# Linear attention and mixture of experts on one core: router in four column groups, part of the first two batches' masks and remainders on ScalarE and GpSimd, batch 0 loaded in halves

## What is computed

```python
x = L0_attn_x                                  # (16, 512, 256)
x = x + attn(layernorm(x), Wq, Wk, Wv, Wo)
x = x + ffn(layernorm(x), ...)

# attn: 16 heads of 16; q, k = elu(proj) + 1; v = proj
#   kv_sum += k_i v_i^T ; k_sum += k_i
#   out_i = (q_i kv_sum) / (q_i . k_sum + 1e-8) ; return out @ Wo.T

# ffn: 8 routed experts of width 128 and one shared one
scores   = sigmoid(x @ gate_w.T)               # 8 per token
scores_c = scores + correction_bias
# the best 2 of 4 pairs of experts, then the best 4 experts of those
topk_w   = chosen scores / their sum * 2.5
out      = sum_e cw[e] * (silu(x @ Wg[e]) * (x @ Wu[e])) @ Wd[e] + shared expert
```

## Time and profile before

| | |
|---|---|
| median of 3 runs | 1066.31 us (1066.13 to 1067.27) |
| the profiled execution's own time | 1064.54 us |
| its span, first to last instruction | 1062.7 us |
| PE busy | 1035.6 us, 97% |
| DVE busy | 857.4 us, 81% |
| POOL, ACT busy | 515.6 and 421.1 us, 49% and 40% |
| granted TensorE clock | 0.998 of full speed over the span |

### The profile page before, as it was taken

The page is one execution under the profiler, slowest core; times in us unless marked ns, Lnnn a source line. Parts: engine busy times, 40 slices in busy tenths (PEclk is TensorE's granted clock), DMA queues, the critical chain, the costliest instruction groups (busy, mean ns, idle before and its releaser), DMA issues.

```text
span 1062.7 us, 22269 instructions
## 1 busy us (share of the span) xinstructions
PE 1035.6 (97%) x8481; PEld 878.6 (83%) x8481; DVE 857.4 (81%) x1856; ACT 421.1 (40%) x751; POOL 515.6 (49%) x423
## 2 busy tenths in 40 slices
PE   7899999999999999999999999999999999999998
PEld 6777888888788888878888887888878888888887
DVE  5999978798787979878798897879978798786553
ACT  5544342443435244352443434334342443431222
POOL 4223435535355463544635355463544645353556
PEclk9999999999999999999999999999999999999999
DMA  6001424444252453324434252453425444240512
GB/s 222 2 21 52 99 57 124 81 110 100 56 135 61 110 119 91 100 54 136 82 110 101 56 134 60 110 120 84 106 50 141 81 110 101 56 113 24 135 40 85
DMA packets 234889, 96.46 MB, mean 91 GB/s; under 512 B 161440, under 2 KB 217248, under 8 KB 234784
## 3 DMA queue, kind: packets, MB, share of 16 engines
q1 hardware_dynamic: 234784, 95.04, 35.5%
HBM read 66.57 MB, written 28.44 MB: 89 GB/s over the span
## 4 chain that ended last, share of the span: by engine, by line
PE 48%; DVE 9%; DMA 6%; issue 5%; POOL 4%; ACT 3%; SPq 1%; DVEq 0%; ACTq 0%; POOLq 0%
PE bank L918 30%; PE y_bank L918 11%; PE bank L1025 3%; DMA x_dram<-blocks 2%; PE bank L1039 2%; POOL h_lo L683 2%; DMA expo<-x_dram 2%; POOL et L679 1%; DVE stats L698 1%; ACT h_hi L637 1%; SPq L496 1%; DVE blocks L778 1%; PE bank L1012 1%; DMA cw_all<-cw_dram 1%; DVE et L895 1%
## 5 line engine op out<-in xcount | busy, mean ns | idle before, releaser
L683 POOL TENSOR_TENSOR h_lo<-et,h_hi 128x512 fp32r<-128x512 f32 x144 | 183.2, 1287 | 169.6 <-ACT h_hi L637 169.2
L918 PE MATMUL bank<-xt_hi,wg_hi 128*128 128x512 f32 x576 | 234.6, 407 | 0.5 <-DVE scores L805 0.3
L918 PE MATMUL bank<-xt_hi,wg_lo 128*128 128x512 f32 x576 | 228.9, 397 | 0.0
L918 PE MATMUL bank<-xt_lo,wg_hi 128*128 128x512 f32 x576 | 227.4, 395 | 0.0
L679 POOL TENSOR_TENSOR et<-et,cw_all 128x512 f32<-128x512 f32 x128 | 164.5, 1292 | 99.5 <-DVE et L901 66.1
L805 DVE TENSOR_TENSOR scores<-bank,cst 128x512 f32<-128x512 f32 x256 | 163.9, 679 | 25.4 <-PE bank L1025 20.5
L637 ACT ACTIVATE h_hi<-et 128x512 fp32r<-128x512 f32 x144 | 88.6, 627 | 212.7 <-POOL et L679 184.8
L918 PE MATMUL y_bank<-wd_hi,h_hi 128*128 128x256 f32 x576 | 164.8, 286 | 0.1
L895 DVE SCALAR_TENSOR_TENSOR et<-et,bank 128x512 f32<-128x512 f32 x144 | 97.0, 682 | 81.1 <-ACT et L628 79.7
L918 PE MATMUL y_bank<-wd_lo,h_hi 128*128 128x256 f32 x576 | 161.1, 280 | 0.0
L918 PE MATMUL y_bank<-wd_hi,h_lo 128*128 128x256 f32 x576 | 161.0, 280 | 0.0
(11 more groups left out here) (130 smaller groups left out, 1918.2 us busy)
## 6 DMA issues: line engine op xcount, KB each, us to landing
cw_all<-cw_dram SPq DMA_DIRECT2D x128, 256.0 KB, 3.7
x_dram<-blocks SPq DMA_DIRECT2D x112, 128.0 KB, 3.3
x_in<-in_x SPq DMA_DIRECT2D x16, 512.0 KB, 5.2
out_y<-x_mid SPq DMA_DIRECT2D x32, 256.0 KB, 3.8
num_t<-x_dram SPq DMA_DIRECT2D x15, 512.0 KB, 4.0
expo<-x_dram SPq DMA_DIRECT2D x13, 512.0 KB, 4.1
k_dram<-blocks SPq DMA_DIRECT2D x52, 96.0 KB, 2.7
k_tok<-k_dram SPq DMA_DIRECT2D x13, 384.0 KB, 3.4
```

Source lines behind the costliest of these rows:

```text
L683: nc.gpsimd.tensor_tensor(h_lo[:, i % HR, :], et[:, i % ET, :], h_hi[:, i % HR, :].bitcast(f32), ALU.subtract).then_inc(h_lo_done, 1)
L918: ins = nc.tensor.matmul(dst, l, r, start=first and n == 0, stop=last and n == 2, skip_group_check=shared)
```

## The change

- The router's matrix (padded with zeros from 8 to 32 columns, `wr`, whole fp32) is now the weights, and the transposed tokens move: one matmul for each block of tokens and half of the features, each block in its own column group, 32 rows of the bank. From batch 1 on the tokens are read whole from `landed[1]` (the tile num_t, as the DMA left it): 8 matmuls. In batch 0, which PE transposes, `xt_hi` and `xt_lo` are read as fp32 one after the other: 16 matmuls. `spread`, which overwrites num_t, waits for the router too.
- DVE turns the bank's 128x128 into `logit` by 32x32 transposes, and `cw` (padded to 32 columns a block, zeroed once by POOL) into `cw_t` (128x128) in the same way at the end of `rank1`. The step `weights_turn` is gone on PE and ACT. The store is 64 KB instead of 16; a load reads four pieces of 512 B for each partition instead of one of 2 KB.
- The tile of equalities (`eq`) is gone: it is written into `cmp` and multiplied there.
- In batches 0 and 1 the masks 1, 3, ... 15 are a copy by ACT, which frees the bank, and the multiplication by POOL from SBUF. `values` waits for both. `at_lo` of these two batches is made by POOL.
- Piece 1's low part goes from DVE to POOL. Batch 0 is loaded by two DMAs of 256 KB, and the statistics of the first half start on the first.
- The tables of order and of banks are others, all through. PE's `warm` transposes are 68 instead of 79.

```diff
@@ FIRST, "PE" @@
-        turn.0.0 turn.1.0 warm.21.0 q.0.0 k.0.0 q.1.0 v.1.0 warm.9.0 k.1.0 scores.0.0 warm.12.0 v.0.0
-        k_turn.1.0 scores.1.0 warm.8.0 turn.0.1 state.1.0 k_turn.0.0 state.0.0 values.0.0 turn.1.1 warm.9.0
-        inter.0.0 scores.2.0 inter.1.0 values.1.0 scores.3.0 k.0.1 k.1.1 values.2.0 values.3.0 inter.2.0
-        inter.3.0 q.0.1 wo.0.0 wo.1.0 q.1.1 scores.0.1 v.1.1 k_turn.0.1 v.0.1 warm.8.0 turn.2.0 turn.3.0
+        turn.0.0 turn.1.0 warm.17.0 k.0.0 q.0.0 k.1.0 v.0.0 q.1.0 k_turn.0.0 k_turn.1.0 v.1.0 scores.0.0
+        warm.10.0 scores.1.0 turn.1.1 state.0.0 warm.10.0 values.0.0 turn.0.1 inter.0.0 scores.2.0 inter.1.0
+        k.0.1 state.1.0 k.1.1 values.1.0 scores.3.0 warm.9.0 q.0.1 values.2.0 inter.2.0 inter.3.0 k_turn.0.1
+        values.3.0 q.1.1 scores.0.1 v.1.1 scores.1.1 wo.0.0 wo.1.0 v.0.1 scores.2.1 values.0.1 k_turn.1.1
+        warm.11.0 turn.3.0 turn.2.0 values.1.1 scores.3.1 router.0.0 warm.11.0 state.0.1 gate.2.0 gate.0.0
...
@@ load of batch 0 @@
+                    sp.dma_start(x_in[0][:, 0:HALF, :], x_v[0][:, 0:HALF, :]).then_inc(x_half, 16)
+                    sp.dma_start(x_in[0][:, HALF:SUBS, :], x_v[0][:, HALF:SUBS, :]).then_inc(x_loaded[0], 16)
@@ cw_load @@
-                    sp.dma_start(cw_all[:, i % CW, :], cw_dram[b % 2, i].partition_broadcast(P))\
+                    sp.dma_start(cw_all[:, i % CW, :].rearrange("p (g t) -> p g t", t=P),
+                                 cw_dram[b % 2].rearrange("(g e) t -> e g t", e=RG)[i].partition_broadcast(P))\
@@ ACT @@
+                elif name == "mask":
+                    act.wait_ge(filled, FILLED["scores", i, b])
+                    nc.scalar.activation(scores[:, i % SM, :, :].rearrange("p h q -> p (h q)"),
+                                         bank[BANK["scores", i]][:, :], ACT.Copy)\
+                        .then_inc(drained[BANK["scores", i]], 1)
@@ POOL @@
+                elif name == "mask":
+                    pool.wait_ge(drained[BANK["scores", i]], USES["scores", i, b])
+                    nc.gpsimd.tensor_tensor(scores[:, i % SM, :, :], scores[:, i % SM, :, :],
+                                            causal.unsqueeze(1).broadcast_to([P, 4, P]), ALU.mult).then_inc(masked, 1)
+                elif name == "at":
+                    nc.gpsimd.tensor_tensor(at_lo[:, i, :], num_t[:, i, :], at_hi[:, i, :].bitcast(f32), ALU.subtract)\
+                        .then_inc(at_lo_pool, 1)
@@ DVE, router and rank1 @@
-                    nc.vector.tensor_reduce(
-                        logit[:, :, :].rearrange("p s e -> p (s e)"),
-                        bank[BANK["router", 0]][:, 0:SUBS * 2 * E].rearrange("p (s t e) -> p s e t", s=SUBS, t=2),
-                        AX.X, ALU.add).then_inc(drained[BANK["router", 0]], 1)
+                    nc.vector.transpose(logit[:, :, :].rearrange("p s e -> p (s e)"), bank[BANK["router", 0]][:, 0:P])\
+                        .then_inc(drained[BANK["router", 0]], 1)
+                    nc.vector.transpose(cw_t[:, :], cw[:, :, :].rearrange("p s e -> p (s e)")).then_inc(cw_turned, 1)
@@ PE, router @@
-                            nc.tensor.matmul(dst, XT[0][:, kc, ss],
-                                             wr_parts[:, kc, :, :].rearrange("p t e -> p (t e)"),
-                                             start=(s == 0 and kc == 0), stop=False, skip_group_check=True)
-                            last = nc.tensor.matmul(dst[:, 0:E], XT[1][:, kc, ss], wr_parts[:, kc, 0, :],
-                                                    start=False, stop=(kc == KC - 1), skip_group_check=True)
+                    whole = [t.bitcast(f32) for t in (XT[0][:, :, :], XT[1][:, :, :])] if b in TURNED[1] else [None]
+                    for n, src in enumerate(whole):
+                        for kc in range(KC):
+                            for s in range(SUBS):
+                                rhs = landed[1][:, s, kc, :] if src is None else src[:, kc, s * P:(s + 1) * P]
+                                last = nc.tensor.matmul(bk[RG * s:RG * s + RG, 0:P], wr[:, kc, :], rhs,
+                                                        start=(n == 0 and kc == 0),
+                                                        stop=(n == len(whole) - 1 and kc == KC - 1),
+                                                        skip_group_check=True)
-                elif name == "weights_turn":
```

336 lines of the change are left out of this document (172 added, 164 removed).

## The result

| | before | after |
|---|---|---|
| median of the runs | 1066.22 us (1064.5 to 1067.27) | 1311.15 us (1306.06 to 1316.3) |
| the profiled execution | 1064.5, span 1062.7 | 1306.65, span 1304.9 |
| granted TensorE clock, mean of the span | 0.998 of 2.4 GHz | 0.915 of it |

After over before is 1.230, with a 95% interval of 1.223 to 1.237. The forecast was 1042 us and 0.92 for faster; the kernel is 245 us slower, and 258 us beyond the end of the range. No rival comes near it.

The account below looks back on a forecast made before the run. PE was taken as the bound, busy 97% of the span, with DVE binding from 27 to 133 us. 20.6 + 1.9 - 3.4 + 1.2 + 3.5 = 23.8 us off 1064.5 gives 1040.7, forecast as a 1042 us median, range 1030 to 1053.

Parts of the forecast that it names:

- Term 6: Batch 0 in halves, and cw_all loads in 512 B pieces: nothing (halves plus or minus 0.4 us), loads hidden behind PE.
- term 1: Router's matmuls on PE: column groups run side by side, 1.32 us less in each of 15 batches, together 20.6 us gained.
- as long as the others keep up: Steady stage: PE time taken away is worth its full length, provided the other engines keep up.
- Term 2: weights_turn gone from PE: 1.9 us gained; DVE's added 0.3 us of work a batch costed at nothing.
- Term 3: New order on PE: two more fp32 runs a batch, 0.12 us each in 14 batches, a loss of 3.4 us.
- its sign of being wrong here: New order: wrong if the period is shorter by 1.5 us or by under 1 us.
- rival B: PE's remaining waits go too, with the new tables and banks: 1029 us; chance 0.17 for anything under 1034.
- Term 4: Eleven fewer warm transposes on PE at 0.11 us each: 1.2 us gained.
- Term 5: The start: DVE sheds masks and remainders, the wait before wo of batch 0 goes: 3.5 us gained.
- Rival C: DVE's masks become the wait before values: 1067 us or more, chance 0.04; milder lateness, 1049 to 1056, 0.11.
- Rival D: POOL is late in the start, wo of batch 0 waits again: 1047 us; chance 0.07.
- Rival A: Router's column groups do not run side by side, its matmuls stay at 1.79 us: 1065, no change; chance 0.04.

Follow-up runs that it names:

- a_order: The changed kernel with SP's repeated order alone altered: cw_load.5 goes behind get.2 of the next batch, loads stay in 512 B pieces; 1225.29 us, ratio 1.151.
- b_pieces: The change's router, cw_t and batch 0 loads with the tables and banks of before (less weights_turn), loads in 512 B pieces; 1300.94 us, ratio 1.222.
- f_best: The changed kernel with each expert's weights stored as one row of 2 KB, run again in more rounds; 1045.55 us, ratio 0.980.
- b_contig: The change's router, cw_t and batch 0 loads with the tables and banks of before (less weights_turn), loads in rows of 2 KB; 1059.2 us, ratio 0.994.
- f_slowrouter: The changed kernel with rows of 2 KB, plus twelve identity transposes ahead of each router's matmuls; 1052.04 us, ratio 0.987.
- a_contig: The changed kernel with the store writing each expert's 512 weights in a row, so loads read one 2 KB piece per partition; 1040.0 us, ratio 0.977.
- e_dvemasks: The changed kernel with rows of 2 KB, masks and attention remainders of batches 0 and 1 back on DVE; 1051.12 us, ratio 0.988.

## Why the prediction was wrong, by its steps

**Term 6 failed, and with it the forecast.** It said "Nothing, hidden behind PE" of the loads in pieces. The reason given was that `num_t<-x_dram` is cut the same way and lands in 4.0 us. It is cut the same way, and that was the trap: there each partition reads pieces of its own, here all read the same four. The comparison was of packet size, and packet size is innocent (3.9 us at 1 KB apart). Place was not compared. A row which does what the new load does, 128 partitions reading four places 16 KB apart, did not exist in the trace, so the term had no upper bound from rows; it deserved a rival, as an operation not shown. The measured price was 5.3 us a load.

The second half of the step was wrong by itself: "if they took 1 us more, only the first `weigh` of a batch would see it". The loads share SP's queue with the puts and gets of k and of the layernorm blocks, and those are on the path. With the issue stalls the wait came out at PE's `state`, 11 us a batch. a_order shows how much of that is the queue's order: 85 of 271 us. The consumer's side was cheap in the step too. In b_pieces, where k comes back in time, the late `weigh` holds ACT's queue, and PE's `state` waits 9.4 us a batch for the `v_win` behind it. The step looked neither at the load's neighbours in the queue nor at what stands behind its reader.

**The sum of the others** came out: 23.8 us forecast, 21.9 measured (f_best's ratio, with rows of 2 KB; 17.8 to 25.9). The parts did not: term 1 was too large, terms 3 and 5 too low, and the errors nearly cancel. That is luck.

- **Term 1, the router, 20.6 us.** The size is right to the rows (0.46 us, 1.3 a batch, in quiet batches the whole of it). What failed is "as long as the others keep up". PE busy at 99% of a stage says that PE sets the pace; it does not say by how much. In both orders the next bound is the round trip of the first layernorm through DRAM. In the old one it stood so near, by way of ACT and DVE, that 6.5 us of 22.5 were left (b_contig); in the new one it shows as the wait for `xa_lo`, and 8.3 us of 21 are what the router is worth (f_slowrouter against f_best, by the ratios).
- **Term 2**, DVE's 0.3 us more a batch, was costed at nothing. Its 128x128 transpose takes 0.31 us, near the 0.25 taken. It was not tried alone. DVE's 4.1 us and more of idle time ahead of each of b_contig's waits speak against it as their cause.
- **Term 3, the new order, a loss of 3.4 us.** Wrong in sign. f_slowrouter has a router as dear as before and from batch 1 to 15 needs 872.2 us, the kernel before 879.7: 7.5 us less, of which `weights_turn` is 1.7. From 212 to 850 us PE idles 1.1 us in it, against 6.4. In quiet batches a_contig's period is 2.0 us shorter than before (61.6 against 63.6), past the 1.5 that the prediction had set as its sign of being wrong here. The switches of precision that I counted may be there, but what the order does is to take waits away, which is what rival B said. B's 1029 did not come about, since others came.
- **Term 4, fewer transposes,** was not tried alone.
- **Term 5, the start, 3.5 us.** Probably too small: 8.8 by e_dvemasks, though in the new order and not in the old, and with an interval that does not quite exclude 3.5. And read wrongly: I capped it at PE's idle time and expected that to fall to near 3 us, but PE idles 6.7 us from 27 to 133 us in a_contig, as before (6.1). The gain is in that it has 996 records done there instead of 963, and comes to `wo` of batch 1 at 102.5 us instead of 109.6. Idle time in a stretch is no ceiling where the `warm` transposes count as busy, and where what fills the stretch is taken from the batches behind.
- **Rival C**, late masks: in f_best's list of PE's waits the masks release 1.9 us on the bank of a projection in the start and 0.7 at `state`; it has no wait of `values` on them. It did not happen. **Rival D** did not happen either: `wo` of batch 0 starts without a wait. It was nearer than term 5 had it: in a_contig POOL ends the second remainder at 51.47 us, not near 44 (the term's own figures add up to 41.7), and PE comes at 53.49. The rival's 4 us counted the masks of both batches, of which only those of batch 0 stand ahead of that `wo`. **Rival A** is refuted by the sixteen records in 0.46 us; the cost of true fp32 that the Trainium skill, "FP8 and Floating Point Precision", section "TensorE Precision Notes", states did not eat up the gain.

One warning could have been found. The Trainium skill, "DMA: Bandwidth & Descriptors", section "Latency and other measured facts", has copies of 128 partitions slow down with the rows of the partitions 2 MiB and more apart, at large powers of two, and come back with padding. The case is another one, and its figures do not carry over. Here partitions 64 KB apart are quick (3.4 us), the distances that hurt are 8 and 16 KB between places that all share, and 512 B of padding are enough, where there 192 B were not and 4 KiB were. The remedy is the same, and it could have led to the right experiment.

## What to carry to other kernels

A DMA is like another only if size, place and readers are alike. Before a layout change in DRAM is costed at nothing, write down for both the piece, the distance and how many read each place, and keep a broadcast read in one run, or pad it off the distances that were slow here (8 and 16 KB, in part 4 KB). Price a slower DMA by what stands in its queue and by what stands behind its reader: the change lost its time by the first road, b_pieces as much by the second. And where an engine is at 99%, ask how far behind it the next chain stands, and follow a wait back beyond the engine that is named: here 1.3 us a batch were enough to meet a read from DRAM, behind DVE in one order and behind POOL in the other.

The version that beats both kernels is the change with rows of 2 KB: 0.980 of the kernel before [0.976, 0.983], 1045.55 us. One padding row per group (d_pitch16k5, 1045.45 us, 0.980 [0.976, 0.984]) is as good with a single store.
